# The expert stage of a decoder layer written out tile by tile

## The chip, the cores and the metric

The program runs on one core of one Trainium2 chip. A core has five engines that run side by side and wait for one another on semaphores: PE (TensorE, matrix multiply), DVE (VectorE), ACT (ScalarE), POOL (GpSimd) and SP (SyncE, which here only issues transfers). A matmul on PE first loads its stationary operand; the profile lists these weight loads apart, as PEld. The metric is the time of one execution on the device, in microseconds (us).

## The reference

The input x is 32 sequences of 128 positions by 128 features. The layer is an attention block (layer norms, a continued-fraction scan, a fast-weight attention with 8 heads, a feed-forward of width 512), a cross attention with 16 heads, and a mixture of experts. Each block is followed by a layer norm over the sum with its input. The change touches the mixture of experts alone:

```
logits = x @ Wr.T ; probs = softmax(logits)
top_v, top_i = top_k(probs, 2) ; top_v = top_v / sum(top_v)
for e in range(8):
    w_e = sum(where(top_i == e, top_v, 0))
    h = gelu(x @ W1[e].T + b1[e])        # 128 -> 512
    y = h @ W2[e].T + b2[e]              # 512 -> 128
    out = out + y * w_e
```

All of it is in float32. There are 4096 positions, and each goes to two of the eight experts: 8192 rows.

## The kernel before

**Stages.** A set-up (to about 110 us) computes what depends on x alone. A loop of 8 passes (to about 641 us) takes 4 sequences a pass through both attentions and the router; at the end of a pass POOL writes the routed rows to a buffer in HBM, `expert_in`, where the rows of one expert stand together. Then comes the **expert stage**, 72 tiles of 128 rows (TILES = 64 + 8, since each expert's last tile may be part full), and after it a closing stage that reads each position's two results back, weighs and sums them, and normalises.

**One tile.** Each tile belongs to one expert, whose number stands in a table in SBUF, `tab`, that is filled while the kernel runs. For tile j:
- SP loads the 128 rows (`row_in`, line 485) and the places where their results belong (`home_of`, line 491).
- PE turns the tile (`turn_rows`, line 1767: a transpose by a matmul), DVE copies the turned tile from PSUM to SBUF (`turned_rows`, line 1353).
- DVE copies the expert's first weights and its bias column, 516 floats a partition, from the table of all experts to one of two buffers `w1c` (`weights`, line 1359; the profile calls that buffer qT).
- PE multiplies (`hidden`, line 1774: four matmuls), ACT applies gelu (`gelu`, line 670: four activations of 128 by 128), PE multiplies by the second weights, read in place at the address of the expert (`outputs`, line 1783: four matmuls that add up in one bank).
- DVE adds the bias b2 of the expert and writes the result to SBUF (`results`, line 1367; the profile calls it xa), and POOL scatters the rows to `expert_out` in HBM (`results_out`, line 858).

**The order.** It is written by hand, each engine's program apart. In step j PE does turn(j+2), hidden(j+1), outputs(j); DVE does turned_rows(j+2), weights(j+2), results(j); ACT does gelu(j); POOL does results_out(j). SP issues the rows of tile j once tile j-4 has been turned, and four row buffers hold them. Turned tiles, w1c, the gelu's output and the PSUM banks are in pairs.

**Loops and numbers.** PE runs its steps in a hardware loop of 17 turns with four steps each, DVE in one of 16 turns with four steps, ACT in one of 3 turns with 24, POOL in one of 9 with 8, SP in one of 8 with 8.
Of the kernel before, what the change touches and what calls it, by code (L numbers as in the profile page):

```python
# [16 lines left out]
P = 128  # L17
# [59 lines left out]
def bass_decoder(nc, A):  # L77
    ctx = ExitStack()
    with ctx:
# [456 lines left out]
        def _(act):  # L536
# [129 lines left out]
            def gelu(j, n):  # L666
                act.wait_ge(h_mm, j + 1 + 2)
                act.wait_ge(y_mm, j + 1)
                for c in range(FC):
                    ins = nc.scalar.activation(hx[n][:, c, :], bank[2 + n][:, c * P:(c + 1) * P], ACT.Gelu,  # L670
                                               bias=w1c[n][:, FF + c:FF + c + 1])
# [39 lines left out]
        def _(pool):  # L711
# [142 lines left out]
            def results_out(j, n, first):  # L854
                pool.wait_ge(y_added, j + 1 + 2)
                pool.wait_ge(home_in[n], first)
                pool.sem_inc(pool_held, 1)
                nc.gpsimd.indirect_dma_start(  # L858
                    ys[:, :], bass.IndirectOffsetOnAxis(ap=home[:, n, 0:1].bitcast(U32), axis=0),
                    ysb[n % UNROLL], None).then_inc(y_out[n % UNROLL], 16)  # L860
# [43 lines left out]
        def _(dve):  # L904
# [445 lines left out]
            def turned_rows(j, n):  # L1350
                dve.wait_ge(turned, j + 1 + UNROLL)
                dve.wait_ge(h_mm, j + 1)
                nc.vector.tensor_copy(xtT[n], bank[n][:, 0:P]).then_inc(turned_copied, 1)

            def weights(j, n):

                e = dve.value_load(tab[0:1, 0, bass.ds(j, 1)], min_val=0, max_val=EXP - 1)
                dve.wait_ge(gelu_done, j + 1)
                nc.vector.tensor_copy(w1c[n], w1_t[:, bass.ds(e, 1), :].rearrange("p a n -> p (a n)")  # L1359
                                      ).then_inc(w1_in, 1)  # L1360

            def results(j, i, n):
                e = dve.value_load(tab[0:1, 0, bass.ds(j, 1)], min_val=0, max_val=EXP - 1)
                dve.wait_ge(y_mm, j + 1 + 2)
                if i is not None:
                    dve.wait_ge(y_out[n], i * 16 + 16)
                nc.vector.tensor_tensor(ysb[n], bank[4 + n % 2][:, 0:P],  # L1367
# [5 lines left out]
            weights(0, 0)  # L1373
            weights(1, 1)
            turned_rows(0, 0)
            turned_rows(1, 1)
            for n in range(UNROLL):
                turned_rows(n + 2, n % 2)
                weights(n + 2, n % 2)
                results(n, None, n)  # L1380
            with dve.Fori(0, TILES // UNROLL - 2) as i:
                for n in range(UNROLL):
                    turned_rows(i * UNROLL + (UNROLL + n + 2), n % 2)
                    weights(i * UNROLL + (UNROLL + n + 2), n % 2)
                    results(i * UNROLL + (UNROLL + n), i, n)
            for n in range(UNROLL):
                j = TILES - UNROLL + n
# [28 lines left out]
        def _(pe):  # L1416
# [347 lines left out]
            def turn_rows(j, i, n):  # L1764
                pe.wait_ge(x_in[n], i * 16 + 16)
                pe.wait_ge(turned_copied, j + 1)
                nc.tensor.transpose(bank[n % 2][:, 0:P], xt[n], ident[:, :]).then_inc(turned, 1)

            def hidden(j, n):
                pe.wait_ge(turned_copied, j + 1 + 2)  # L1770
                pe.wait_ge(w1_in, j + 1)
                pe.wait_ge(gelu_done, j + 1)
                for c in range(FC):
                    ins = mm(bank[2 + n % 2][:, c * P:(c + 1) * P], w1c[n % 2][:, c * P:(c + 1) * P],  # L1774
                             xtT[n % 2], start=True, stop=True)
                ins.then_inc(h_mm, 1)

            def outputs(j, n):
                e = pe.value_load(tab[0:1, 0, bass.ds(j, 1)], min_val=0, max_val=EXP - 1)
                pe.wait_ge(gelu_done, j + 1 + 2)  # L1780
                pe.wait_ge(y_added, j + 1)
                for c in range(FC):
                    ins = mm(bank[4 + n % 2][:, 0:P], hx[n % 2][:, c, :],  # L1783
# [4 lines left out]
            turn_rows(0, 0, 0)  # L1788
            turn_rows(1, 0, 1)
            hidden(0, 0)  # L1790
            with pe.Fori(0, TILES // UNROLL - 1) as i:
                for n in range(UNROLL):
                    ahead = n + 2
                    turn_rows(i * UNROLL + ahead, i + ahead // UNROLL, ahead % UNROLL)
                    hidden(i * UNROLL + (n + 1), n + 1)
                    outputs(i * UNROLL + n, n)
            for n in range(UNROLL):
                j = TILES - UNROLL + n
                if j + 2 < TILES:
                    turn_rows(j + 2, (j + 2) // UNROLL, (j + 2) % UNROLL)  # L1800
                if j + 1 < TILES:
                    hidden(j + 1, n + 1)
# [75 lines left out]
```

## Time and profile before

| | us |
|---|---|
| median of 3 runs | 866.14 (862.64 to 867.37) |
| the profiled execution, its time | 862.9 |
| its span, from first to last instruction | 861.0 |
| granted TensorE clock, mean over the span | 0.907 |
| busy: PE 667.3 (78%), weight loads 480.8 (56%), DVE 537.5 (62%), ACT 378.1 (44%), POOL 367.9 (43%) | |
| first row tile turned | 658.58 |
| last `results` of the expert stage | 813.47 |

The expert stage thus takes about 155 us of the 861. A row of the timeline gives the start in us from the span's start, the duration in us, the engine, the line, the operation, what it writes and reads, how many instructions are merged in the row, and in brackets the idle time of the engine before it and what ended it.
### The profile page before, as it was taken

To read this page: it belongs to the slowest core of one execution; us is meant where nothing else is said; L and a number is where in the kernel's file an instruction comes from. 1 tells how busy PE (TensorE), PEld (TensorE's weight loads), DVE (VectorE), ACT (ScalarE), POOL (GpSimd) and SP (SyncE) were. 2 spreads that over 40 slices of the span, in tenths; PEclk is the share of its full clock that TensorE was granted. 3 is DMA by queue.
4 is the path that set the end of the run, shared out by engine and by line. 5 is a ranking of instruction groups with operands and counts; after the bars stand their busy time and mean duration, and the time that the engine had idled before them with its cause. 6 is when DMAs were issued, how large, how long until landed. Compare 5 with 4: busy or idle time off the path is not lost.

```text
span 861.0 us, 21597 instructions
## 1 busy us (share of the span) xinstructions
PE 667.3 (78%) x6159; PEld 480.8 (56%) x6160; DVE 537.5 (62%) x1725; ACT 378.1 (44%) x798; POOL 367.9 (43%) x514
## 2 busy tenths in 40 slices
PE   4325988978988888978988988988963999999700
PEld 1212645744744754754753763754653999989700
DVE  3585567678677677677677776676673444444343
ACT  2002164354454454454454444444521555555455
POOL 2524172254255155156056056057033555455555
PEclk9555998999999999999999999999895999999955
DMA  7500000000000000000000000001204222222153
GB/s 252 203 0 13 1 30 11 2 22 16 0 19 19 0 19 19 0 19 19 0 19 19 0 19 19 0 4 34 71 31 95 63 65 65 62 59 65 47 171 122
DMA packets 45528, 36.43 MB, mean 42 GB/s; under 512 B 20059, under 2 KB 39452, under 8 KB 45249
## 3 DMA queue, kind: packets, MB, share of 16 engines
q1 hardware_dynamic: 37312, 23.09, 9.6%
q0 software_dynamic: 4608, 9.59, 3.3%
q10 hardware_dynamic: 3584, 3.48, 1.2%
q8 instruction: 9, 0.15, 0.1%
q14 instruction: 15, 0.12, 0.0%
HBM read 23.35 MB, written 12.76 MB: 42 GB/s over the span
## 4 chain that ended last, share of the span: by engine, by line
PE 47%; DVE 19%; issue 12%; POOL 11%; ACT 4%; DMA 3%; DVEq 1%; POOLq 1%; SPq 0%; ACTq 0%
PE bank L1783 8%; PE bank L1774 8%; PE bank L1492 8%; PE bank L1529 5%; POOL rstd L769 4%; PE bank L1650 3%; POOL expert_in L798 3%; PE bank L1637 2%; DVE negmax L1179 2%; PE bank L1619 2%; PE bank L1577 2%; DVE stats L1063 2%; PE bank L1658 2%; DVE xn L1072 2%; PE bank L1585 1%
## 5 line engine op out<-in xcount | busy, mean ns | idle before, releaser
L766 POOL TENSOR_SCALAR vare<-mv 128x1 f32<-128x1 f32 (+1 forms) x112 | 25.6, 229 | 279.6 <-DVE mv L1068 277.6
L858 POOL DMA_INDIRECT expert_out<-xa,home x72 | 80.1, 1112 | 81.0 <-DVE xa L1367 44.4
L670 ACT ACTIVATE hT<-bank,qT 128x128 f32<-128x128 f32 x288 | 81.7, 369 | 63.1 <-PE bank L1774 61.9
L1783 PE MATMUL bank<-w_t,hT 128*128 x576 | 80.6, 283 | 3.9 <-ACT hT L670 3.9
L798 POOL DMA_INDIRECT expert_in<-xb_rows,slot_u x72 | 73.8, 1025 | 22.4 <-issue 17.4
L1179 DVE TENSOR_REDUCE negmax<-bank 128x4 f32<-128x512 f32 x128 | 79.4, 683 | 3.9 <-PE bank L1619 3.1
L565 ACT ACTIVATE mix<-bank 128x512 f32<-128x512 f32 x128 | 66.1, 603 | 33.6 <-PE bank L1637 32.0
L1774 PE MATMUL bank<-xnT,qT 128*128 128x128 f32 x576 | 79.8, 283 | 0.1
L1492 PE MATMUL bank<-xqT,w_qkv 128*128 128x512 f32 x144 | 73.0, 623 | 5.1 <-DVE x L1168 5.1
L1783 PEld LDWEIGHTS bank<-w_t,hT 128*128 128x128 f32 x576 | 69.9, 191 | 6.4 <-issue 4.9
L1774 PEld LDWEIGHTS bank<-xnT,qT 128*128 128x128 f32 x576 | 71.5, 195 | 3.2 <-issue 2.6
L769 POOL TENSOR_TENSOR rstd<-vare,minus_half 128x1 f32<-128x1 f32 (+1 forms) x112 | 67.6, 604 | 9.9 <-POOL vare L766 0.9
L1112 DVE TENSOR_TENSOR hT<-bank,decay 128x512 f32<-128x512 f32 x72 | 46.4, 686 | 28.1 <-PE bank L1529 28.0
L1359 DVE COPY qT<-w_t 128x516 f32 x72 | 31.0, 431 | 43.9 <-issue 39.6
L565 ACT ACTIVATE hebT<-bank 128x512 f32<-128x512 f32 x36 | 21.5, 597 | 64.5 <-PE bank L1577 64.5
L1367 DVE TENSOR_TENSOR xa<-bank,b_bc 128x128 f32<-128x128 f32 x72 | 21.0, 292 | 41.8 <-PE bank L1783 29.5
L1492 PE MATMUL bank<-w_qkv,xqT 128*128 128x512 f32 x72 | 42.0, 673 | 5.7 <-ACT mix L565 5.2
L1529 PE MATMUL bank<-qT,kT 64*128 64x128 f32 x576 | 41.8, 285 | 1.5 <-DVE hT L1112 1.4
L1492 PEld LDWEIGHTS bank<-xqT,w_qkv 128*128 128x128 f32 x144 | 25.7, 197 | 29.9 <-issue 22.2
L565 ACT ACTIVATE cT<-bank 128x512 f32<-128x512 f32 x32 | 19.1, 597 | 52.2 <-PE bank L1650 52.2
L1650 PE MATMUL bank<-mix,vpad 128*32 128x128 f32 x1024 | 36.7, 287 | 6.3 <-DVE hT L1112 5.4
L1492 PE MATMUL bank<-xnT,w_ff 128*128 128x512 f32 x64 | 37.5, 742 | 4.9 <-ACT xnT L565 4.9
(290 smaller groups left out, 1399.3 us busy)
## 6 DMA issues: line engine op xcount, KB each, us to landing
xn<-expert_in SPq DMA_DIRECT2D x72, 64.0 KB
mix<-expert_out SPq DMA_DIRECT2D x8, 512.0 KB, 4.0
ctxT<-in_ctxT SPq DMA_DIRECT2D x9, 256.0 KB
w_t<-in_w_t ACTq DMA_DIRECT2D x1, 2064.0 KB, 7.8
xT_all<-in_xT SPq DMA_DIRECT2D x4, 512.0 KB, 5.6
x_all<-in_x SPq DMA_DIRECT2D x4, 512.0 KB, 9.2
w_t<-in_w_t SPq DMA_DIRECT2D x1, 2048.0 KB, 7.8
expert_in<-xb_rows,slot_u POOLq DMA_INDIRECT x72
```

What stands on the lines that cost most here:

```text
L565: nc.scalar.activation(dst, src_ap, func, scale=scale, **kw).then_inc(free[BANK[name]], 1)
L670: ins = nc.scalar.activation(hx[n][:, c, :], bank[2 + n][:, c * P:(c + 1) * P], ACT.Gelu, bias=w1c[n][:, FF + c:FF + c + 1])
L769: nc.gpsimd.tensor_tensor(rstd[stage][:, t:t + n], vare[stage][:, t:t + n], minus_half[:, 0:n], ALU.pow).then_inc(rstd_ready[stage], n)
L798: nc.gpsimd.indirect_dma_start(xs[:, :], bass.IndirectOffsetOnAxis(ap=slot_u[:, t, k:k + 1], axis=0), xb_rows[k][:, t, :], None).then_inc( ...
L858: nc.gpsimd.indirect_dma_start(ys[:, :], bass.IndirectOffsetOnAxis(ap=home[:, n, 0:1].bitcast(U32), axis=0), ysb[n % UNROLL], None).then_i ...
L1112: nc.vector.tensor_tensor(at[t % 2][:, r, :, :], b[:, :].rearrange("p (a n) -> p a n", a=PAIRS), decay[:, t, :].unsqueeze(1).broadcast_to( ...
L1179: nc.vector.tensor_reduce(negmax[t % 2][:, i, 28:28 + XC], b[:, :].rearrange("p (c n) -> p c n", c=XC), AX.X, ALU.max, negate=True).then_i ...
L1492: done(mm(b[:, :], lhsT, rhs, start=True, stop=True), name)
L1529: ins = mm(halves[r][:, tile(p)], kT[rows, p, tile(t)], qT[rows, p, tile(t)], start=True, stop=True)
L1650: ins = mm(b[32 * i:32 * i + 32, tile(c)], vpad[:, t, 4 * c + i, :], pT[t % 2][:, i, c, :], start=True, stop=True)
L1774: ins = mm(bank[2 + n % 2][:, c * P:(c + 1) * P], w1c[n % 2][:, c * P:(c + 1) * P], xtT[n % 2], start=True, stop=True)
L1783: ins = mm(bank[4 + n % 2][:, 0:P], hx[n % 2][:, c, :], w2_t[:, bass.ds(e, 1), c, :].rearrange("p a n -> p (a n)"), start=(c == 0), stop=( ...
```

## The change

The four loops of the expert stage on PE, DVE, ACT and POOL are gone: each step is an instruction sequence of its own, with j a constant. With that:
- semaphore targets are constants, and the register instructions that computed them go;
- DVE reads an expert's number once, in `weights`, and keeps it in a register until `results` two steps later;
- PE waits for one semaphore in each of its three parts: `turn_rows` no longer waits for turned_copied, `hidden` no longer for turned_copied and gelu_done, `outputs` no longer for y_added but in the last tile. (What they guarded is covered through w1_in, h_mm and gelu_done, since DVE and ACT work in order.)

SP's program, its loop too, is as before, and so is the work on tiles and numbers. The core of the diff:

```diff
-            in_turn = 6 * UNROLL
-            with act.Fori(0, TILES // in_turn) as i:
-                for n in range(in_turn):
-                    gelu(i * in_turn + n, n % 2)
+            for j in range(TILES):
+                gelu(j)
...
-            with pool.Fori(0, TILES // (2 * UNROLL)) as i:
-                for n in range(2 * UNROLL):
-                    results_out(i * (2 * UNROLL) + n, n, i * 16 + 16)
+            for j in range(TILES):
+                results_out(j)
...
-            def weights(j, n):
-
-                e = dve.value_load(tab[0:1, 0, bass.ds(j, 1)], min_val=0, max_val=EXP - 1)
+            def expert_of(j):
+                return dve.value_load(tab[0:1, 0, j:j + 1], min_val=0, max_val=EXP - 1)
+
+            def weights(j, e):
+
                 dve.wait_ge(gelu_done, j + 1)
...
-            def results(j, i, n):
-                e = dve.value_load(tab[0:1, 0, bass.ds(j, 1)], min_val=0, max_val=EXP - 1)
+            def results(j, e):
                 dve.wait_ge(y_mm, j + 1 + 2)
-                if i is not None:
-                    dve.wait_ge(y_out[n], i * 16 + 16)
...
+                if j >= UNROLL:
+                    dve.wait_ge(y_out[j % UNROLL], 16 * (j // UNROLL))
...
+            experts = [expert_of(0), expert_of(1)]
+            weights(0, experts[0])
+            weights(1, experts[1])
+            turned_rows(0)
+            turned_rows(1)
+            for j in range(TILES):
                 if j + 2 < TILES:
-                    turned_rows(j + 2, n % 2)
-                    weights(j + 2, n % 2)
-                results(j, TILES // UNROLL - 2, n)
+                    turned_rows(j + 2)
+                    experts.append(expert_of(j + 2))
+                    weights(j + 2, experts[j + 2])
+                results(j, experts[j])
...
-            def turn_rows(j, i, n):
-                pe.wait_ge(x_in[n], i * 16 + 16)
-                pe.wait_ge(turned_copied, j + 1)
...
-            def hidden(j, n):
-                pe.wait_ge(turned_copied, j + 1 + 2)
+            def hidden(j):
                 pe.wait_ge(w1_in, j + 1)
-                pe.wait_ge(gelu_done, j + 1)
...
-            def outputs(j, n):
-                e = pe.value_load(tab[0:1, 0, bass.ds(j, 1)], min_val=0, max_val=EXP - 1)
+            def outputs(j):
+                e = pe.value_load(tab[0:1, 0, j:j + 1], min_val=0, max_val=EXP - 1)
+                if j + 1 == TILES:
+                    pe.wait_ge(y_added, j + 1)
                 pe.wait_ge(gelu_done, j + 1 + 2)
-                pe.wait_ge(y_added, j + 1)
```

How the instructions stand now. On PE, one step of the expert stage before (REGISTER_ALU and ISA are register work or waits of the sequencer; bank2 takes the result of `hidden`, bank5 that of `outputs`, whose three further matmuls are left out):

```order
L1767 MATMUL bank1<-ident,xn 128x128 [waits turned_copied,x_in3]
L1770 REGISTER_ALU
L1774 MATMUL bank2<-xnT,qT 128x128 [waits gelu_done,w1_in,turned_copied]
L1774 MATMUL bank2<-xnT,qT 128x128 x3
L1779 ISA
L1779 TENSOR_LOAD tab
L1779 ISA x2
L1783 ISA [waits y_added,gelu_done]
L1783 MATMUL bank5<-w2_t,hT 128x128
```

and a step at the same place now:

```order
L1756 MATMUL bank0<-ident,xn 128x128 [waits x_in2]
L1761 MATMUL bank3<-xnT,qT 128x128 [waits w1_in]
L1761 MATMUL bank3<-xnT,qT 128x128 x3
L1766 TENSOR_LOAD tab
L1766 ISA x2
L1771 ISA [waits gelu_done]
L1771 MATMUL bank4<-w2_t,hT 128x128
```

Four waits and two register instructions are gone from the step; the matmuls and the load of the expert's number stand as they stood.

On DVE, one step before (xnT is the turned tile, qT the buffer w1c, xa the result):

```order
L1352 REGISTER_ALU [waits turned]
L1353 COPY xnT<-bank0 128x128 [waits h_mm]
L1357 ISA
L1357 TENSOR_LOAD tab
L1357 ISA x2
L1359 ISA [waits gelu_done]
L1359 COPY qT<-w1_t 128x516
L1363 TENSOR_LOAD tab
L1363 ISA x2
L1367 ISA [waits y_out2,y_mm]
L1367 TENSOR_TENSOR xa<-bank4,b2_bc 128x128
L1351 REGISTER_ALU
```

and now:

```order
L1350 COPY xnT<-bank0 128x128 [waits h_mm,turned]
L1353 TENSOR_LOAD tab
L1353 ISA x2
L1358 ISA [waits gelu_done]
L1358 COPY qT<-w1_t 128x516
L1365 ISA [waits y_out2,y_mm]
L1365 TENSOR_TENSOR xa<-bank4,b2_bc 128x128
```

The second load, between the copy of the weights and the addition of the bias, is gone with its two register instructions, and so are the register instructions ahead of the waits.

On ACT, the start of the stage before (ACT_TABLE_LOAD puts the table of the gelu in place):

```order
L675 UNCONDITIONAL_BRANCH
L675 ISA
L668 REGISTER_ALU [waits h_mm]
L670 ACT_TABLE_LOAD
L670 ACTIVATE hT<-bank2,qT 128x128 [waits y_mm]
```

and now:

```order
L670 ACT_TABLE_LOAD [waits y_mm]
L670 ACTIVATE hT<-bank2,qT 128x128 [waits h_mm]
L670 ACTIVATE hT<-bank2,qT 128x128 x3
L670 ACTIVATE hT<-bank3,qT 128x128 [waits y_mm,h_mm]
```

The table load stood behind the wait for the first `hidden` (h_mm) and inside the loop's body, so that it ran once in each of the three turns; now it stands once, ahead of that wait, behind a semaphore (y_mm) that PE raises before its first tile.

## Rows read from the trace of the kernel before

**Rows 1.** Windows: busy us by engine, PE clock, DMA share, GB/s, expert stage

```profile
664.00:812.00 148.00, 144.75 (x1197) 139.12 (x1197) 65.85 (x210) 83.16 (x287) 78.02 (x70) 1.00 0.25 62
```

**Rows 2.** Timeline of PE's weight loads: steps inside the loop

```profile
748.21 0.14 PEld L1767 LDWEIGHTS bank<-ident,xn 128*128 128x128 f32 x1
748.32 0.97 PEld L1774 LDWEIGHTS bank<-xnT,qT 128*128 128x128 f32 x8
749.21 0.97 PEld L1783 LDWEIGHTS bank<-w_t,hT 128*128 128x128 f32 x8
750.10 0.14 PEld L1767 LDWEIGHTS bank<-ident,xn 128*128 128x128 f32 x1
750.28 0.97 PEld L1774 LDWEIGHTS bank<-xnT,qT 128*128 128x128 f32 x8
```

**Rows 3.** The same view: turns of the fourth tile and of the last

```profile
665.18 0.14 PEld L1767 LDWEIGHTS bank<-ident,xn 128*128 128x128 f32 x1
...
807.74 0.14 PEld L1767 LDWEIGHTS bank<-ident,xn 128*128 128x128 f32 x1
```

**Rows 4.** Timeline of DVE, the same steps

```profile
746.30 0.29 DVE L1367 TENSOR_TENSOR xa<-bank,b_bc 128x128 f32<-128x128 f32 x1 [0.49 <-issue]
...
748.73 0.29 DVE L1367 TENSOR_TENSOR xa<-bank,b_bc 128x128 f32<-128x128 f32 x1 [0.67 <-issue]
748.94 0.28 DVE L1353 COPY xnT<-bank 128x128 f32<-128x128 f32 x1
749.78 0.43 DVE L1359 COPY qT<-w_t 128x516 f32 x1 [0.56 <-issue]
750.70 0.29 DVE L1367 TENSOR_TENSOR xa<-bank,b_bc 128x128 f32<-128x128 f32 x1 [0.49 <-PE bank L1783]
```

**Rows 5.** DVE's sequencer by line: count, min/median/max ns, first and last start

```profile
L1363 DVEq TENSOR_LOAD <-tab x72: 298/304/327, 664.2 to 811.9; - x72
L1366 DVEq EVENT_SEMAPHORE  x52: 21/21/21, 675.7 to 812.9; - x52
```

**Rows 6.** PE's sequencer, the waits ahead of `hidden`

```profile
L1772 PEldq EVENT_SEMAPHORE  x72: 51/179/487, 659.2 to 809.1; - x72
```

**Rows 7.** Timeline of DVE behind its loop, where j is a constant

```profile
806.52 0.29 DVE L1353 COPY xnT<-bank 128x128 f32<-128x128 f32 x1
807.29 0.43 DVE L1359 COPY qT<-w_t 128x516 f32 x1 [0.47 <-issue]
```

**Rows 8.** ACT's table loads by line, and PE's waits for ACT in the timeline

```profile
L670 ACT ACT_TABLE_LOAD  x3: 1283/1283/1283, 661.6 to 763.4; - x3
...
664.30 1.15 PE L1783 MATMUL bank<-w_t,hT 128*128 x8 [0.98 <-ACT hT L670]
...
759.22 1.15 PE L1783 MATMUL bank<-w_t,hT 128*128 x8 [1.48 <-ACT hT L670]
```

**Rows 9.** PE's instruction fetches (queue, packets, MB, share), window 111 to 175 us

```profile
q8 instruction: 5, 0.08, 0.5%
```

**Rows 10.** Timeline of PE: first and last work of the first and second pass

```profile
111.38 3.67 PE L1492 MATMUL bank<-xnT,w_ff 128*128 128x512 f32 x8 [0.78 <-ACT xnT L565]
...
175.05 0.18 PE L1743 MATMUL bank<-chosen,tri_b 128*128 128x32 bf16 x1
...
175.99 3.67 PE L1492 MATMUL bank<-xnT,w_ff 128*128 128x512 f32 x8 [0.59 <-ACT xnT L565]
...
241.21 0.18 PE L1743 MATMUL bank<-chosen,tri_b 128*128 128x32 bf16 x1
```

**Rows 11.** Timeline: SP's first row loads, the first turn, and a later row load

```profile
656.73 2.14 SPq L485 DMA_DIRECT2D xn<-expert_in  x4
658.58 0.18 PEld L1767 LDWEIGHTS bank<-ident,xn 128*128 128x128 f32 x1 [17.41 <-DMA xn<-expert_in]
...
748.81 0.33 SPq L485 DMA_DIRECT2D xn<-expert_in  x1
```

**Rows 12.** The same view: PE turns the tile of that later row load

```profile
754.24 0.14 PEld L1767 LDWEIGHTS bank<-ident,xn 128*128 128x128 f32 x1
```

More of the change, by code:

```diff
@@ L664, in _, with gelu @@
             act.sem_inc(gelu_done, 2)
-            def gelu(j, n):
+            def gelu(j):
                 act.wait_ge(h_mm, j + 1 + 2)
@@ L1372, in _ @@
             dve.wait_ge(experts_loaded, 16 * len(EXPERT_LOADS))
[L1373 to L1387, printed above, removed]
+            experts = [expert_of(0), expert_of(1)]
[4 more added lines that the diff above has]
+            for j in range(TILES):
                 if j + 2 < TILES:
-                    turned_rows(j + 2, n % 2)
-                    weights(j + 2, n % 2)
-                results(j, TILES // UNROLL - 2, n)
+                    turned_rows(j + 2)
+                    experts.append(expert_of(j + 2))
+                    weights(j + 2, experts[j + 2])
+                results(j, experts[j])
             def combine(g, m):
@@ L1762, in _, with turn_rows @@
             pe.sem_inc(y_mm, 2)
-            def turn_rows(j, i, n):
-                pe.wait_ge(x_in[n], i * 16 + 16)
-                pe.wait_ge(turned_copied, j + 1)
-                nc.tensor.transpose(bank[n % 2][:, 0:P], xt[n], ident[:, :]).then_inc(turned, 1)
-            def hidden(j, n):
-                pe.wait_ge(turned_copied, j + 1 + 2)
+            def turn_rows(j):
+                pe.wait_ge(x_in[j % UNROLL], 16 * (j // UNROLL + 1))
+                nc.tensor.transpose(bank[j % 2][:, 0:P], xt[j % UNROLL], ident[:, :]).then_inc(turned, 1)
+            def hidden(j):
                 pe.wait_ge(w1_in, j + 1)
-                pe.wait_ge(gelu_done, j + 1)
                 for c in range(FC):
-                    ins = mm(bank[2 + n % 2][:, c * P:(c + 1) * P], w1c[n % 2][:, c * P:(c + 1) * P],
-                             xtT[n % 2], start=True, stop=True)
+                    ins = mm(bank[2 + j % 2][:, c * P:(c + 1) * P], w1c[j % 2][:, c * P:(c + 1) * P],
+                             xtT[j % 2], start=True, stop=True)
                 ins.then_inc(h_mm, 1)
-            def outputs(j, n):
-                e = pe.value_load(tab[0:1, 0, bass.ds(j, 1)], min_val=0, max_val=EXP - 1)
+            def outputs(j):
+                e = pe.value_load(tab[0:1, 0, j:j + 1], min_val=0, max_val=EXP - 1)
+                if j + 1 == TILES:
+                    pe.wait_ge(y_added, j + 1)
                 pe.wait_ge(gelu_done, j + 1 + 2)
-                pe.wait_ge(y_added, j + 1)
                 for c in range(FC):
-                    ins = mm(bank[4 + n % 2][:, 0:P], hx[n % 2][:, c, :],
+                    ins = mm(bank[4 + j % 2][:, 0:P], hx[j % 2][:, c, :],
                              w2_t[:, bass.ds(e, 1), c, :].rearrange("p a n -> p (a n)"), start=(c == 0),
@@ L1786, in outputs @@
                 ins.then_inc(y_mm, 1)
[L1788 to L1798, printed above, removed]
+            turn_rows(0)
+            turn_rows(1)
+            pe.wait_ge(turned_copied, 2 + 2)
+            hidden(0)
+            for j in range(TILES):
                 if j + 2 < TILES:
-                    turn_rows(j + 2, (j + 2) // UNROLL, (j + 2) % UNROLL)
+                    turn_rows(j + 2)
                 if j + 1 < TILES:
-                    hidden(j + 1, n + 1)
-                outputs(j, n)
+                    hidden(j + 1)
+                outputs(j)
 def host_layout(inp):
```

20 lines of the change are left out of this document (10 added, 10 removed).

## The prediction

> **What bounds the kernel now.** The change lies in the expert stage, so the stage comes first. The windows view gives 144.8 us of PE busy and 139.1 us of weight loads in the 148 us from 664 to 812, at a granted clock of 1.00, which is the upper level (2.4 GHz); DVE is busy for 65.9, ACT for 83.2, POOL for 78.0 [rows 1]. PE seems to be the bound, but a busy PE can still be one that is fed late, so the second view is its weight loads in order of time. A full-speed step reads: turn at 748.21, `hidden` at 748.32, `outputs` at 749.21, next turn at 750.10 [rows 2]. That is 1.89 us, 0.11 + 0.89 + 0.89, with the loads back to back. No step can be shorter while the matmuls are what they are, and none of them is touched. The mean step is longer: from the turn of the fourth tile, 665.18, to that of the last, 807.74, are 68 steps in 142.56 us, 2.10 us each [rows 3]. So 68 x (2.096 - 1.89) = 14.0 us of the stage are not PE's own work.
>
> Who takes them? The third view is DVE's timeline. From one `results` to the next DVE needs 748.73 to 750.70, 1.97 us, and the step across the loop's turn, 746.30 to 748.73, took 2.43 [rows 4]. DVE computes for only 0.29 + 0.28 + 0.43 = 1.00 us of it. The rest is "issue": 0.56 us before the copy of the weights and 0.49 before `results`. Both gaps hold the load of an expert's number, 304 ns, and its register work [rows 5]. That the 0.49 is named as a wait for PE misleads: the sequencer's wait instruction at that place lasts 21 ns at minimum, median and maximum, all 52 times, so PE's result was always there when DVE asked [rows 5]. PE in turn waits ahead of `hidden`, with a median of 179 ns and a minimum of 51 [rows 6]; the weights that it waits for are done at 749.78 + 0.43 = 750.21, and `hidden` starts at 750.28 [rows 2, 4]. So DVE's sequencer paces the steps and PE follows it, with PE's floor 10% below.
>
> **The change part by part.** *DVE, the second load of the number.* It removes one load with its register work from each step. Behind the loop, with j a constant, xnT to the copy of the weights takes 807.29 - 806.52 = 0.77 us [rows 7] instead of 749.78 - 748.94 = 0.84 [rows 4]. The new step is then 0.21 (xa to xnT, 748.73 to 748.94) + 0.77 + 0.43 (the copy) + a wait and one register instruction. Without the load, the last part lies between 0 and the 0.49 that it is now; I take 0.1, since the 0.49 holds 0.30 of load and more of its register work. The sum is 1.51 us, at most 1.90. DVE stops being the bound.
>
> *DVE's and PE's loops and register instructions.* The 2.43 across a loop's turn is 0.46 above the 1.97 of a step inside, 16 times; that is part of the 14.0 us and goes with it. PE's register instructions and four waits per step lie behind its own queue of matmuls, and cost nothing by themselves in the 1.89 us step [rows 2].
>
> *What is late next.* With DVE freed, the weights for a step are ready along this chain, from the turn's weight load at T: `results` starts at T + 0.52 and xnT at T + 0.73 in the step where T = 748.21, the weights start 0.77 later and take 0.43, T + 1.93, and `hidden` followed them by 0.07, so T + 2.00 [rows 2, 4, 7]. PE itself would be there at T + 1.89 + 0.11 = T + 2.00. The two meet. I take 1.90 us for a step; the lower end is 1.89, the upper end 1.97 (the same chain with the old 0.84, T + 2.07, as the trace has it).
>
> *ACT's loop.* The table load of 1.28 us ran three times [rows 8] and now runs once, ahead of the wait for `hidden`. The two in mid-stage are within the 14.0 us. The first one stood between the first `hidden` and its gelu, and PE then sat idle for 0.98 us before its first `outputs` at 664.30 [rows 8], which is outside the 68 steps. I take 0.9 for it; it is between 0 (another wait of the start takes over) and 0.98.
>
> *POOL's loop.* POOL is busy for 78.0 of 148 us [rows 1], and its transfers wait for DVE; I cost its edit at nothing, covered by PE's steps. If that cover went, its register work could cost some tenths in a step, which is in the third case below.
>
> *A stall that isn't the change's.* PE sat idle for 1.48 us before 759.22 [rows 8], once, at no table load and no loop's turn. I can't tie it to anything that is removed and leave it in: 1.5 us, with the rest of that step 1.7.
>
> *The sum*, against the profiled execution: 68 x (2.096 - 1.90) = 13.3, minus 1.7 for the stall that stays, plus 0.9 at the start: 12.5 us. Its span of 861.0 becomes 848.5, its time of 862.9 becomes 850.4. It ran 3.2 us below the median of the runs, 866.1; since runs after will scatter in the same way, I take the sum off the median: 866.1 - 12.5 = 853.6 us.
>
> **A cost that the trace doesn't show.** PE's program in the stage grows from a loop's body to straight code, which has to be fetched. Of fetching there is one good witness, the first pass over the main loop: its code came in by 5 fetches in the 64 us from 111 to 175, which took 0.5% of 16 engines' time, 5.1 us, or 1.0 each [rows 9]. From its first feed-forward matmul to its last ranking matmul that pass took 175.05 - 111.38 = 63.7 us, the second pass 241.21 - 175.99 = 65.2 [rows 10]. The fetched pass was no slower, so the fetches hid. At that pace the stage has 137 / 12.8 = some 11 fetches. Bounds for one: 0, and 2.9 us if PE stood still for the whole of it (1.0 and the 1.85 us that the first row load took from issue, 656.73, to the turn, 658.58 [rows 11]). I take 0, as the passes show, and keep both ends: 0 to 32 us.
>
> The Trainium skill (Runtime: NRT & Kernel Launch, Instruction fetch mechanics) says that the sequencer streams straight code ahead by itself at a mostly hidden cost, while a taken branch to code outside the window stalls until it is fetched. By this rule the cost above is about 0, and full unrolling is the better form. The passes of rows 10 agree with the first half; of the second the rows show nothing. The skill also warns (DMA: Bandwidth & Descriptors, Latency and other measured facts) of a floor of some 600 ns for a load of a register. The trace has 304 [rows 5], and the measurement decides; by the skill's figure the removed part would be larger, but PE's floor would take the surplus.
>
> **The rivals.** *B, the chain of the weights becomes the new wait.* What speaks for it: it meets PE's floor with no slack by my own sum, so 0.07 us more in it, in every step, shows in full. Against: the wait is now on the first matmul of `hidden` alone, so that PE's sequencer may read its next number meanwhile. At 1.97 us: 68 x (2.096 - 1.97) = 8.6, - 1.7 + 0.9 = 7.8, giving 858.3 us.
>
> *C, the row loads become the bound.* SP's program is unchanged, loop and all. If its present pace, the steps' 2.10 us, were its own limit and not that of its surroundings, then PE could run ahead only as far as the rows lie ready. The rows issued at 748.81 were turned at 754.24, 5.4 us later [rows 11, 12], and need 1.85; so 3.6 us of gain and the 0.9, giving 861.6 us. The same holds for a limit on POOL. Against it: SP issued four row loads in 2.14 us at the start [rows 11].
>
> *D, slower: the fetches of PE's code don't hide.* The stage differs from the first pass in that its DMA share is 0.25 [rows 1] and PE has no gaps in which a late fetch could be lost. It decides at the point where 11 fetches cost more than the gain and 0.5% of the time: (12.5 + 4.3) / 11 = 1.5 us each. With the 1.85 us of a landing each, 20.4 us: 866.1 - 12.5 + 20.4 = 874.0 us.
>
> **How the numbers follow.** Forecast (PE at its floor, 1.89 to 1.93): 0.70, 850 to 857. B: 0.15. C: 0.08. D: 0.07. This kernel's measurement tells about 0.5% from no change, here 4.3 us: faster means below 861.8. The forecast and B are faster, and C with a quarter of its chance: 0.87. The same: 0.07, the rest of C and mild forms of D. Slower: 0.06. The range reaches from 850 (floor at 1.89, the stall gone, 866.1 - 14.0 - 0.98 = 851.1, and 1 us of scatter) over B to 861.
>
> **What would show it.** Right: the turns follow at 1.89 to 1.90 us from the fourth tile to the last, with no period of four; DVE's gap before `results` is named as a wait for PE and is a real one, and its register load runs 72 times instead of 144 between its two places; one table load, before the first `hidden`; no idle of PE before the first `outputs`. The stage from the fourth turn to the last takes 129 to 131 us. B shows as idle weight loads before `hidden` behind the copy of the weights, in each step; C as PE waiting for xn; D as PE idle with nothing named, at the times of the fetches, some 12 us apart. The forecast is wrong if the steps stay above 1.97 us on average.

## The result, and the profile after

The kernel after takes 860.29 us (median of 17 runs, 853.72 to 873.2), the kernel before on the same chip 866.14 (17 runs, 860.4 to 874.28): ratio 0.993, 95% interval 0.9909 to 0.9952. (The chip has a second, slower state, and the ratio leaves out runs in it; 873.2 is one.) It is faster by 5.9 us; 12.5 us were forecast. The direction held, the size did not. Its profiled execution took 856.75 us with a span of 854.9 and a mean clock of 0.913.

The windows view of the kernel after, expert stage:

```profile
658.00:806.00 148.00, 140.92 (x1196) 134.91 (x1195) 65.71 (x209) 80.91 (x284) 71.06 (x70) 1.00 0.26 63
```

PE is busy for 141 of 148 us where it was 145 [rows 1], at the same clock: in this execution it idles more than before. The timeline of PE's weight loads shows where. At first the stage runs as forecast, with 1.89 to 1.90 us from turn to turn (one step of the first 14 has 2.08):

```profile
658.96 0.14 PEld L1756 LDWEIGHTS bank<-ident,xn 128*128 128x128 f32 x1
...
678.10 0.14 PEld L1756 LDWEIGHTS bank<-ident,xn 128*128 128x128 f32 x1
678.22 0.97 PEld L1761 LDWEIGHTS bank<-xnT,qT 128*128 128x128 f32 x8
...
680.00 0.14 PEld L1756 LDWEIGHTS bank<-ident,xn 128*128 128x128 f32 x1
```

From tile 18 on (tiles are counted from 0) it doesn't. The same view, later:

```profile
688.03 0.14 PEld L1756 LDWEIGHTS bank<-ident,xn 128*128 128x128 f32 x1 [0.36 <-DMA xn<-expert_in]
...
710.12 0.14 PEld L1756 LDWEIGHTS bank<-ident,xn 128*128 128x128 f32 x1 [0.73 <-DMA xn<-expert_in]
...
738.78 0.14 PEld L1756 LDWEIGHTS bank<-ident,xn 128*128 128x128 f32 x1 [1.01 <-DMA xn<-expert_in]
...
752.19 0.14 PEld L1756 LDWEIGHTS bank<-ident,xn 128*128 128x128 f32 x1 [1.28 <-DMA xn<-expert_in]
...
801.80 0.14 PEld L1756 LDWEIGHTS bank<-ident,xn 128*128 128x128 f32 x1
```

PE waits for the rows of the tile. The last turn at 801.80 makes 142.84 us for the 68 steps, as much as before (142.56, [rows 3]). The summary of waits (engine and line, releaser, sum in us, times, longest) for PE's weight loads, 658 to 806 us:

```profile
PEld bank L1756 <- DMA xn<-expert_in: 8.5, 15, 1.3
PEld bank L1756 <- issue: 1.8, 5, 0.8
PEld bank L1771 <- issue: 0.4, 1, 0.4
PEld bank L1761 <- DVE qT L1358: 0.2, 1, 0.2
```

For the kernel before the same summary (664 to 809 us) has no wait for rows at all:

```profile
PEld bank L1783 <- issue: 4.2, 4, 1.7
PEld bank L1774 <- issue: 2.6, 16, 0.2
```

And the chain that ended last, on the page of the kernel after, now runs over SP's issues in the stage (L472 loads a row number, L485 and L491 issue the two transfers):

```profile
PE 31%; DVE 20%; issue 17%; POOL 12%; SPq 12%; DMA 3%; ACT 3%; DVEq 1%; POOLq 1%; ACTq 0%
PE bank L1482 7%; PE bank L1519 5%; POOL rstd L767 4%; SPq L491 4%; SPq L472 3%; PE bank L1640 3%; DVE negmax L1176 3%; POOL expert_in L796 3%; SPq L485 3%; PE bank L1627 2%; PE bank L1567 2%; DVE stats L1060 2%; PE bank L1609 2%; PE bank L1648 2%; ACT mix L565 2%
```

SP issues the rows of tile j once tile j-4 is turned. It was 2.9 us behind that turn at tiles 9 to 12 and 5.8 to 8.5 behind from tile 31 on, mostly 6.6 to 7.1 (rows of tile 12 issued at 671.53, turn of tile 8 at 668.62; rows of tile 71 at 800.04, turn of tile 67 at 793.24). It no longer waits for that turn: it is late by its own work. That is rival C.

Where this one pair of executions differs by 6.1 us of span is another matter. The first turn came at 652.24 instead of 658.58, from code that the change doesn't touch, where PE's clock has short stretches at the lower level: its mean over 100 to 650 us was 0.97, and 0.96 before. A second execution of the kernel before, below, had 0.97 too and its first turn at 653.35. In the stage itself this pair shows no gain (142.84 against 142.56). So the 5.9 us rest on the timed medians, and the explanation on the steps of this and the following runs.

### The profile page after: what moved, and what is told of

It reads as the page before. It is cut to its first block, busy times and chain, and to the rows that moved or that the text cites. A ratio compares the mean times of both kernels' runs of the same rounds, so it can differ in the third digit from the quotient of the medians.

```text
span 854.9 us, 20569 instructions
## 1 busy us (share of the span) xinstructions
PE 658.6 (77%) x6159; PEld 472.4 (55%) x6159; DVE 536.8 (63%) x1724; ACT 376.3 (44%) x796; POOL 360.8 (42%) x514
## 4 chain that ended last, share of the span: by engine, by line
PE 31%; DVE 20%; issue 17%; POOL 12%; SPq 12%; DMA 3%; ACT 3%; DVEq 1%; POOLq 1%; ACTq 0%
PE bank L1482 7%; PE bank L1519 5%; POOL rstd L767 4%; SPq L491 4%; SPq L472 3%; PE bank L1640 3%; DVE negmax L1176 3%; POOL expert_in L796 3%; SPq L485 3%; PE bank L1627 2%; PE bank L1567 2%; DVE stats L1060 2%; PE bank L1609 2%; PE bank L1648 2%; ACT mix L565 2%
## 5 line engine op out<-in xcount | busy, mean ns | idle before, releaser
L856 POOL DMA_INDIRECT expert_out<-xa,home x72 | 73.1, 1015 | 88.5 <-DVE xa L1365 56.5
L1771 PE MATMUL bank<-w_t,hT 128*128 x576 | 77.0, 277 | 0.7 <-DVE xa L1365 0.5
L1761 PEld LDWEIGHTS bank<-xnT,qT 128*128 128x128 f32 x576 | 73.7, 199 | 0.9 <-DVE xnT L1350 0.7
L1482 PE MATMUL bank<-w_qkv,xqT 128*128 128x512 f32 x72 | 39.6, 639 | 5.7 <-ACT mix L565 5.2
L1756 PE MATMUL bank<-ident,xn 128*128 128x128 f32 x72 | 22.3, 309 | 24.2 <-DMA xn<-expert_in 22.7
L1575 PE MATMUL bank<-w_out,hebT 128*128 128x128 f32 x288 | 40.6, 284 | 0.4 <-DVE hT L1109 0.4
```

Of the source, the lines that this page charges most:

```text
L856: nc.gpsimd.indirect_dma_start(ys[:, :], bass.IndirectOffsetOnAxis(ap=home[:, j % (2 * UNROLL), 0:1].bitcast(U32), axis=0), ysb[j % UNROLL ...
L1482: done(mm(b[:, :], lhsT, rhs, start=True, stop=True), name)
L1575: ins = mm(b[:, 0:P], hebT[t % 2][:, p, :], w_out[:, p, :], start=(p == 0), stop=(p == PAIRS - 1))
L1761: ins = mm(bank[2 + j % 2][:, c * P:(c + 1) * P], w1c[j % 2][:, c * P:(c + 1) * P], xtT[j % 2], start=True, stop=True)
L1771: ins = mm(bank[4 + j % 2][:, 0:P], hx[j % 2][:, c, :], w2_t[:, bass.ds(e, 1), c, :].rearrange("p a n -> p (a n)"), start=(c == 0), stop=( ...
```

## The experiments

Each kernel was timed against the kernel before on its own chip. "Step" is the mean over the 68 steps from the fourth turn to the last in the profiled execution.

| kernel | median us | before, same chip | ratio, 95% interval | step us |
|---|---|---|---|---|
| before, again | 856.38 (1 run) | 857.13 | | 2.073 |
| after, again | 853.85 | 857.54 | 0.9946 [0.9915, 0.9978] | 2.003 |
| one transfer per tile | 843.68 | 857.54 | 0.9824 [0.9776, 0.9872] | 1.905 |
| no scatter | 848.88 | 857.54 | 0.9891 [0.9841, 0.9942] | 2.023 |
| one transfer, old DVE | 852.47 | 857.54 | 0.9938 [0.9902, 0.9974] | 2.004 |
| SP written out | 843.89 | 857.13 | 0.9857 [0.9832, 0.9882] | 1.906 |
| one transfer, number read twice | 843.72 | 857.13 | 0.9863 [0.9836, 0.989] | 1.902 |
| one transfer, all PE waits | 844.15 | 857.13 | 0.9854 [0.983, 0.9878] | 1.906 |
| before, SP written out | 868.95 | 867.23 | 1.003 [0.9998, 1.0062] | 2.096 |
| SP written out, old PE | 854.96 | 867.23 | 0.9875 [0.9822, 0.9928] | 2.010 |
| one transfer, old ACT | 852.47 | 867.23 | 0.9836 [0.9783, 0.9888] | 1.973 |
| one transfer, SP written out | 850.49 | 867.23 | 0.9802 [0.9747, 0.9857] | 1.952 |

Times are compared by ratio, since the kernel before took 866.1, 857.5, 857.1 and 867.2 us on the chips used. SP's issues come late singly in all profiles of the kernel after; where before took 866 they do so more (2.18 us from row issue to row issue, tiles 8 to 71, against 2.06 in the repetition). Where it took 866 or 867, each profile has besides a disturbed place at tile 48 or 49, one step of 3.3 to 3.8 us in all but the last of the table; the last four steps of the table contain it.

**After, again.**

> The changed kernel once more, for a second profile and a second comparison. Theory S (the gain was eaten by SP: its row loads now pace the expert stage): the first 15 or so steps run at 1.89 us, the mean of the 68 steps from the fourth turn to the last is again 2.08 to 2.12 us, PE idles for the rows of tiles, and the time is within 0.993 +- 0.003 of before. Rival N (the first profile was an outlier, the stage normally gains what I forecast): the 68 steps take 1.90 to 1.97 us each, some 10 us less than in the first profile.

Steps of 1.90 alternate with longer ones, two of them 3.42 and 3.50, in which PE waits for rows; the mean is 2.003, between the two that were expected (2.08 to 2.12, 1.90 to 1.97). The timeline of SP shows its pace from one row issue (L485) to the next:

```profile
701.91 0.33 SPq L485 DMA_DIRECT2D xn<-expert_in  x1
702.50 0.33 SPq L491 DMA_DIRECT2D home<-expert_in  x1
703.81 0.33 SPq L485 DMA_DIRECT2D xn<-expert_in  x1
704.40 0.33 SPq L491 DMA_DIRECT2D home<-expert_in  x1
705.72 0.33 SPq L485 DMA_DIRECT2D xn<-expert_in  x1
...
707.69 0.33 SPq L485 DMA_DIRECT2D xn<-expert_in  x1
...
711.61 0.33 SPq L485 DMA_DIRECT2D xn<-expert_in  x1
...
713.93 0.34 SPq L485 DMA_DIRECT2D xn<-expert_in  x1
...
716.06 0.33 SPq L485 DMA_DIRECT2D xn<-expert_in  x1
```

It is 1.90 us in most steps, 1.97 in one, and 2.32 and 2.13 around the loop's turn at 713. Its period of eight is 2.32, 2.09, 1.90, 1.90, 1.91, 1.97, 1.90, 1.90, on average 1.99, above PE's 1.90. That is the undisturbed pace. With the single late issues it was 2.06: rows of tile 8 at 664.02, of tile 71 at 794.07. PE's mean could stay below that, at 2.003, since it used up a head start: SP was 2.8 us behind the turn at tile 9 and 5.9 behind at tile 71. Part of the gain is thus had only once. Before the loop SP needs 1.66 (the kernel after, where SP waits for no scatter and computes no target):

```profile
655.36 0.33 SPq L485 DMA_DIRECT2D xn<-expert_in  x1
655.87 0.33 SPq L491 DMA_DIRECT2D home<-expert_in  x1
657.02 0.33 SPq L485 DMA_DIRECT2D xn<-expert_in  x1
```

The load of the row number alone is one of the costs between (SP's sequencer by line: count, min/median/max ns; kernel after):

```profile
L472 SPq TENSOR_LOAD <-tab x72: 4/268/698, 645.4 to 799.0; - x72
```

**One transfer per tile.** A row of `expert_in` holds its 128 values and, behind them, the place where its result belongs; SP fetches the two by two transfers. Here one does, into eight buffers. With the second transfer goes one of the two waits and its target, and the rows may be fetched up to eight tiles ahead instead of four.

```
-    sp.wait_ge(turned, j + 1)
-    sp.sem_inc(sp_held, 1)
-    sp.dma_start(xt[n % UNROLL], xs[bass.ds(row, P), 0:P]).then_inc(x_in[n % UNROLL], 16)
...
-    sp.dma_start(home[:, n, :], xs[bass.ds(row, P), P:RW]).then_inc(home_in[n], 16)
+    sp.dma_start(rows_in[:, n, :], xs[bass.ds(row, P), :]).then_inc(home_in[n], 16)
```

> The changed kernel with one transfer per tile on SP instead of two: rows and places come together (132 floats a row) into eight buffers, and the second issue of 0.33 us with its wait and register work goes. Theory S: SP needs about 1.1 us a step, PE is never late for rows, all 68 steps run at 1.89 to 1.93 us; the stage loses some 12 us against the changed kernel, and the time comes to about 849 us, 0.980 of before. Rival F (what holds the steps at 2.1 us is PE's code being fetched, or DVE's chain): the steps stay at 2.0 us or more and the time stays within 2 us of the changed kernel.

The step is 1.905 (turns at 657.61 and 787.14), 129.5 us for the stage's 68, inside the 129 to 131 that the prediction gave, and the summary of waits for PE's weight loads in it is empty. In the chain, SP is gone:

```profile
PE 46%; DVE 20%; issue 12%; POOL 12%; DMA 4%; ACT 3%; DVEq 1%; POOLq 1%; SPq 0%; ACTq 0%
```

**No scatter.** POOL issues nothing; writing the results back is left out, and the buffer of results is filled with zeros once, ahead of the stage.

```
-    nc.gpsimd.indirect_dma_start(ys[:, :], ..., ysb[j % UNROLL], None).then_inc(y_out[j % UNROLL], 16)
+    pool.sem_inc(y_out[j % UNROLL], 16)
```

> The changed kernel without POOL's 72 scatters of results in the expert stage (results are not written back; POOL only passes the signal on). SP's program is untouched. Theory S1 (SP is slow because its instructions stand still while POOL prepares a scatter): SP falls back to its pace at the stage's start, 1.66 us a step, and PE runs at 1.89 us; about 849 us. Rival S2 (SP is slow by its own two transfers, whatever POOL does): SP's step stays at 2.0 to 2.1 us and so do PE's; about 860 us less the last scatter, 857 us.

The step stayed at 2.023, and SP's own at 1.90 inside and 2.32 at the loop's turn. Neither POOL nor the traffic of its scatters holds the rows back. The time is 5.0 us below that of the kernel after on this chip (848.88 against 853.85), where S2 had about 3; 2.9 of it is the closing stage's (44.6 us from the last results to the end instead of 47.5), and none comes from the steps.

**SP written out.** Two transfers stay; SP's loop over the last 64 tiles goes.

```
-    with sp.Fori(0, TILES // (2 * UNROLL) - 1) as i:
-        for n in range(2 * UNROLL): ...
+    for j in range(2 * UNROLL, TILES):
+        row = sp.value_load(tab[0:1, 1, j:j + 1], ...)
+        row_in(j, j % (2 * UNROLL), row)
+        home_of(j % (2 * UNROLL), row, 16 * ((j - 2 * UNROLL) // UNROLL + 1))
```

> The changed kernel with SP's loop written out as well: still two transfers a tile, but no register work for targets and indices and no loop's turn. Theory S2 (SP's own chain of instructions is the bound: 1.90 us a step inside the loop, 2.09 to 2.32 at its turn, 1.99 in the mean): the chain falls to 1.66 + 0.13 for the two waits' instructions = 1.79 us, below PE's 1.90, and PE's 68 steps take 1.90 to 1.93 us; about 0.983 of before, equal to the kernel with one transfer within 3 us. Rival Q (the transfers themselves back up, seen as single issues of 0.9 to 1.7 us instead of 0.33): steps stay at 1.97 us or more.

SP's timeline:

```profile
701.95 0.33 SPq L485 DMA_DIRECT2D xn<-expert_in  x1
702.54 0.33 SPq L491 DMA_DIRECT2D home<-expert_in  x1
703.68 0.33 SPq L485 DMA_DIRECT2D xn<-expert_in  x1
```

1.73 us a tile, with the same transfers and the same four buffers. PE steps at 1.906 and waits for nothing. Single issues come late here too (once 3.87 us after the one before), but SP catches up at 1.73. This separates SP's instructions from its transfers: what held the kernel after was register work (indices, wait targets, the loop's turn), 1.99 instead of 1.73.

**One transfer, old DVE.** DVE's code of before, loop and two loads of the number.

```
+    with dve.Fori(0, TILES // UNROLL - 2) as i:
+        for n in range(UNROLL):
+            turned_rows(i * UNROLL + (UNROLL + n + 2), n % 2)
+            weights(i * UNROLL + (UNROLL + n + 2), n % 2)
+            results(i * UNROLL + (UNROLL + n), i, n)
```

> One transfer per tile, but DVE's part of the expert stage as before the change (loop of four steps, the number loaded twice); PE, ACT and POOL written out. It asks whether DVE's sequencer really set the 2.06 us of a step before. If so (my prediction's reading): steps have the period of four again, 2.03 to 2.06 us in the mean, DVE's gap before the bias addition is issue time, and the time is 9 to 11 us above the kernel with one transfer and the new DVE. Rival: if SP set the pace before too, then with SP freed and the old DVE the steps take 1.9 us and the two kernels are equal.

The step is 2.004, in a period of four (2.15, 2.01, 1.97, 1.90): DVE's old code alone, loop and second load together, costs 0.10 a step. That is below the 2.03 to 2.06 that were expected, and so is the time, 8.8 us above the version with DVE's new code, where 9 to 11 were expected (852.47 - 843.68; the steps make 6.8 of it).

**One transfer, number read twice.** DVE's straight code, with the second load put back.

```
     def results(j, e):
+        e = dve.value_load(tab[0:1, 0, j:j + 1], min_val=0, max_val=EXP - 1)
```

> One transfer per tile, all written out, but DVE reads the expert's number twice again. With the old DVE loop the steps took 2.00 us, with the new code 1.905. If the second load is what made DVE slow, DVE's step is now 1.51 + 0.49 - 0.1 = 1.90 to 1.95 us, and PE's steps 1.93 to 1.97, 2 to 4 us more than with one load of the number. If the loop and its register work made it slow, the steps stay at 1.905 and the time is equal within 1 us.

1.902: in straight code the second load costs no time. First DVE's timeline in it, then in the version with DVE's old loop:

```profile
720.53 0.29 DVE L1356 TENSOR_TENSOR xa<-bank,b_bc 128x128 f32<-128x128 f32 x1 [0.56 <-PE bank L1762]
720.74 0.28 DVE L1340 COPY xnT<-bank 128x128 f32<-128x128 f32 x1
721.40 0.43 DVE L1348 COPY qT<-w_t 128x516 f32 x1 [0.38 <-issue]
722.43 0.29 DVE L1356 TENSOR_TENSOR xa<-bank,b_bc 128x128 f32<-128x128 f32 x1 [0.60 <-PE bank L1762]
```

```profile
701.44 0.43 DVE L1346 COPY qT<-w_t 128x516 f32 x1 [0.56 <-issue]
702.28 0.29 DVE L1354 TENSOR_TENSOR xa<-bank,b_bc 128x128 f32<-128x128 f32 x1 [0.41 <-PE bank L1768]
702.76 0.29 DVE L1340 COPY xnT<-bank 128x128 f32<-128x128 f32 x1 [0.19 <-issue]
703.62 0.43 DVE L1346 COPY qT<-w_t 128x516 f32 x1 [0.56 <-issue]
```

With constants, xnT (the copy of the turned tile) to the weights' copy takes 0.66 us although the number is read in between; in the loop 0.84 to 0.86, since the load's index is computed first, and at the loop's turn xa to xnT takes 0.48 instead of 0.21. The gap before `results` (xa) looks alike in both, but only in the first is it a wait for PE. There the sequencer starts the second load with the weights' copy, at 721.42, and is through with it at 722.01, 0.18 us after the copy's end; PE's result comes later still, and `results` starts at 722.43. So the load still lengthens DVE's own chain, and the slack behind it hides that. In the loop there is no such slack: at 702.28 `results` started as soon as the sequencer was through with the load. How much of the loop's cost is the load's, no run tells, since none has the loop with one load. The sequencer's instruction ahead of `results` can't tell: in the version where DVE stands idle for 0.4 to 0.6 us until PE's result, in nearly every step, it reads

```profile
L1355 DVEq EVENT_SEMAPHORE  x68: 21/21/21, 666.9 to 793.7; - x68
```

exactly as before the change [rows 5]. By the semaphores of these records it is the wait for the scatter (y_out), in three of its four buffers before the change and in all four now. The wait for PE (y_mm) leaves no row of its own: it is part of the next record, which lasts 57 ns each time (L1356, 72 times), although DVE waits. These durations don't contain the wait.

**One transfer, all PE waits.** The waits that the change removed, put back as constants.

```
+    pe.wait_ge(turned_copied, j + 1)             # ahead of the turn
+    pe.wait_ge(turned_copied, j + 1 + 2)         # ahead of hidden
...
+    pe.wait_ge(gelu_done, j + 1)
+    pe.wait_ge(y_added, j + 1)                   # ahead of outputs
```

> One transfer per tile, all written out, with PE's four removed waits (turned_copied twice, gelu_done, y_added) back in each step, as constants. Each is satisfied before PE comes to it, so if they only cost sequencer time behind a full queue, the steps stay at 1.905 us and the time is equal within 1 us. Rival: with the wait for w1_in in front as an instruction of its own PE's sequencer can't read the next number meanwhile, 1.02 us from that wait to the first load of outputs against 0.89 of hidden: 0.1 us a step, 2.0 us steps, 7 us more.

1.906, ratio 0.9854, against 0.9863 for the version above on the same chip: "one wait per step on PE" is worth nothing.

**Before, again** (one run).

> The kernel before once more, for a second profile of its expert stage. If DVE's sequencer set its pace, the period of four returns with the same four step times (2.22, 1.90, 2.05, 2.08, in the mean 2.06); 68 steps in 140 to 143 us. If SP set it, the mean moves with SP's stalls as it did between the two profiles of the changed kernel (2.10 and 2.00).

Step 2.073, with the period of four 2.22, 1.90, 2.05, 2.08, the two steps of 2.85 and 2.89 at ACT's table loads, and no stall at tile 48. The profiles of the two kernels on chips where before takes 857 thus differ by 68 x (2.073 - 2.003) = 4.8 us in the stage, of the order of the timed 3.7 (857.54 - 853.85). It doesn't account for the 5.9 timed on the first chip, whose two profiles have the same stage.

**Before, SP written out.**

> The kernel before, with SP's loop over the last 64 tiles written out (two transfers per tile stay). It is the control for the theory that before the change the loops of DVE and PE set the step (2.06 us, period of four 2.22, 1.90, 2.05, 2.08) and SP's 1.99 us per tile was hidden below it. Theory: the mean step stays at 2.05 to 2.09, the period of four stays, the time stays within 0.5% of before (ratio 0.995 to 1.005). Rival (SP's chain already took part in the bound before, since DVE's and SP's long steps add up in places): the mean step falls to 2.00 or less and the time by 4 us or more.

The step is 2.096, the period the same, the ratio 1.003. Before the change SP held nothing back: the same edit that takes the kernel after from 853.85 to 843.89 us (ratio 0.9946 to 0.9857, on two chips) gives the kernel before nothing.

**SP written out, old PE.** PE's loop and waits of before.

> The kernel after with SP's loop written out, and PE's code as it was before the change (its loop of four tiles and its three waits per step). Theory: PE's loop costs only its own turn, once in four tiles, so the mean step goes from 1.906 to 1.93 to 1.96 and the time 1.5 to 4 us above that of the version with SP written out (about 843.9), so about 846. Rival (DVE's loop alone made the step long, PE's sequencer ran ahead of its matmuls and its loop is hidden): the step stays at 1.90 to 1.91, time within 1 us of 843.9.

The steps are 2.22, 1.90, 1.90, 1.90: 1.98 on average and 2.01 with one stall of 3.76. The timeline of its weight loads at a turn of the loop:

```profile
698.75 0.14 PEld L1754 LDWEIGHTS bank<-ident,xn 128*128 128x128 f32 x1
699.04 0.97 PEld L1761 LDWEIGHTS bank<-xnT,qT 128*128 128x128 f32 x8
700.08 0.97 PEld L1770 LDWEIGHTS bank<-w_t,hT 128*128 128x128 f32 x8
700.97 0.14 PEld L1754 LDWEIGHTS bank<-ident,xn 128*128 128x128 f32 x1
```

`hidden` comes 0.29 us after the turn's weight load instead of 0.11, `outputs` 1.04 after that instead of 0.89. I expected 1.93 to 1.96: PE's loop costs 0.32 at each turn, 17 times. PE's queue of matmuls didn't hide it. In time it can't be told from the version without PE's loop (0.9875 and 0.9857, on two chips).

**One transfer, old ACT.** ACT's loop of before, three turns of 24 tiles (the expectation says 12).

> The kernel with one transfer per tile, and ACT's code as it was before the change (loop of 12 tiles, so three loads of ACT's table in the stage). Theory: two steps of the 68 become longer by the table load in them (2.85 us instead of 1.90, so 2 x 0.95), the others stay at 1.90: mean step 1.93, time 1.5 to 2.5 us above the 843.7 of the version with one transfer, and all 71 other steps unchanged. Rival (ACT's loop also delays the gelus at its turns): more than 3 us above.

Two steps of 2.93 at the table loads, 1.03 above the others each, a stall of 3.34 at tile 49, the rest 1.90 but for the first step of 3.03 and a few of 2.01 to 2.05. The mean of 1.973 is above the expected 1.93 by that first step and the stall. In time it can't be told from the version without it (0.9836 and 0.9824, on two chips).

**One transfer, SP written out.**

> The kernel with one transfer per tile and, besides, SP's loop written out. With SP's chain at some 1.1 us per tile in either form, PE's 1.90 us is the bound already. Theory: mean step 1.90 to 1.91, time within 1.5 us of the 843.7 that one transfer alone gives. Rival (what is left of SP's loop still holds single steps back, or instructions fetched for SP take something from others): the mean step 1.88 or lower with 2 us gained, or 2 us lost.

Steps of 1.90, but for a disturbed stretch from tile 48 on (single steps of 2.16 to 2.68); DVE had waited 2.3 us there; by the semaphores it was for PE's result (y_mm), while the scatter's buffer was free. The mean of 1.952 misses the expected 1.90 to 1.91 by this stretch. The ratio, 0.9802, lies within the interval of one transfer alone. Both beat the kernel after, by 1.1 to 1.4%; which is the better isn't told apart.

## Why the prediction was only half right

**The bound of before.** PE's floor of 1.89 us is right: 1.90 in one transfer per tile. "DVE's sequencer paces the steps and PE follows it" was half of it. DVE's old code alone gives 2.004 to 2.007, PE's loop alone 1.98, both together 2.06. PE's register instructions were costed at nothing; they cost 0.32 at each of 17 turns, some 5 us. That didn't hurt the forecast, since both loops went.

**The second load.** I priced it at 0.30 us and more of each step, from a gap that held it and a row of 21 ns that was to show that PE's result was always there. The row is of another wait, for the scatter. In straight code the load costs no time, but only because PE's result comes later than the load is through. In the loop of before it stood in DVE's chain together with the register work, and which of the two made DVE late no run separates. That DVE waited little for PE before is right all the same: by the starts of the sequencer's records 0.03 us in the median step, and 0.13 in the first of each turn of the loop. The row didn't show it.

**What is late next.** The steps stayed above the 1.97 us that the prediction named as the sign of being wrong, with 2.10 and, in the repetition, 2.003. The step that failed is this one: of rival C the prediction says "Against it: SP issued four row loads in 2.14 us at the start", and gives it 0.08. Those are four transfers with their registers ready and no waits [rows 11]. In its loop SP does per tile a load of a number (268 ns), two transfers (333 ns each), two waits and their targets: 1.99 us on average, where I had set 2.14 / 4 = 0.54 against the steps of 1.90. The condition that C names, that SP's pace of before is nearly its own limit, was true: 1.99 of 2.06. C gave 861.6, and 860.29 was measured; the mechanism is C's, but that the numbers lie so near is luck in part, for C's 3.6 us in the stage and 0.9 at its start were nothing in the first pair of profiles. DVE and PE met PE's floor as forecast, in 13 of the first 14 steps of the kernel after and in 63 of 68 with one transfer per tile; B, idle weight loads behind the copy of the weights, appeared once, with 0.16 us.

**The sum.** The term 68 x (2.096 - 1.90) = 13.3 was mis-sized: 68 x (2.073 - 2.003) = 4.8 was had on the chips where before takes 857, and nothing in the first pair of profiles. The rest is SP's: 68 x (2.073 - 1.905) = 11.4 us are there once SP is out of the way. The 0.9 at the start didn't come: the table load moved ahead (644.11), the first gelu followed PE at once, and the weight loads of the first `outputs` came 5.0 us behind the first turn, where its matmuls had come 5.7 behind it [rows 8, 11], but at the lower clock:

```profile
644.11 1.28 ACT L670 ACT_TABLE_LOAD   x1 [8.93 <-issue]
655.80 1.14 ACT L670 ACTIVATE hT<-bank,qT 128x128 f32<-128x128 f32 x4 [10.41 <-PE bank L1761]
```

```profile
657.27 1.77 PEld L1771 LDWEIGHTS bank<-w_t,hT 128*128 128x128 f32 x8
658.96 0.14 PEld L1756 LDWEIGHTS bank<-ident,xn 128*128 128x128 f32 x1
659.07 0.97 PEld L1761 LDWEIGHTS bank<-xnT,qT 128*128 128x128 f32 x8
```

They took 1.77 us instead of 0.97, the upper level (1.00) was granted only from the next tile on, and from the first turn to the fourth it was 6.72 us instead of 6.60. In the other versions with ACT's new code that stretch took 5.9 to 6.9, with its old loop 7.8 in one and 6.6 in the kernel before, so the price of the first table load isn't settled. The stall that I left in is there in the kernel after (3.64 at tile 48), and in none of the profiles from the chips where the kernel before took 857. In all six from the other chips DVE waits 1.9 to 2.3 us there for PE, whose signal for `outputs` comes 1.3 to 1.8 us later than its matmuls end by the (modelled) rows. In all thirteen profiles with scatters, of either kind of chip, POOL issues the scatter of tile 41 some 3.7 us after that of tile 40, where 1.9 is usual, shortly before. What causes either stays open, and so does what delays single issues of SP; by these delays and the stall the profiled execution of the kernel after has a step of 2.10 and its repetition 2.00.

**What was costed at nothing.** POOL's edit: no run has it alone. With POOL's new code the steps reach PE's floor, and with no scatter at all the kernel after is no faster in its steps; what its old loop would cost at 1.90 us a step isn't shown. The fetches of PE's code (the row is of the page of the kernel after; queue, packets, MB, share):

```profile
q8 instruction: 19, 0.31, 0.2%
```

There were 9 before. One transfer per tile has 19 too, 11 of them while its tiles are turned, and none of its 68 steps is longer than 2.06 us, so they hid, and D, which needed 1.5 us each, is out. That agrees with what the prediction cites from the Trainium skill (Runtime: NRT & Kernel Launch, Instruction fetch mechanics).

## What to carry to other kernels

When a change speeds up the engines that pace a loop, count the instructions per step of every other queue that feeds it, transfers, register loads, wait targets and loop turn included, in the steady state and not in the start-up: the queue with the next longest step takes over, here at 1.99 us of the old 2.06. A gap that "contains" an instruction doesn't price it, since the sequencer may do it under the work before or ahead of a wait; put it back alone, and look at the slack behind it. And before a sequencer row is read as "never waits", check which of the waits it is, and whether it gets longer where the engine is known to wait.

## What the runs showed of the hardware

- SP's cost per tile is its instructions: undisturbed 1.99 us in a loop, 1.73 written out, 1.66 without the wait for the scatter, with the same two transfers. With one transfer of 66 KB a tile, the issues followed each other at 1.09 us at the start.
- A loop's turn cost PE 0.32 us, and DVE 0.27 (xa to xnT, 0.48 instead of 0.21). Computed indices and targets added to DVE's gaps as well: with constants the gap before the weights' copy fell from 0.56 to 0.38.
- In the sequencer's rows of DVE the record with the wait for PE lasted 57 ns all 72 times (number read twice), although DVE stood idle for 0.4 to 0.6 us ahead of most of them.
- The same kernel before took 857 us on two chips, and 866 and 867 us in the two other series.
